# Turning attention probabilities by DMA transposes instead of TensorE, from the third pair on, in a decoder layer on one core

## What is computed

```
q, k, v = x @ wq + bq, x @ wk + bk, x @ wv + bv        # 16 heads of 16
scores  = softmax(q k^T / 4)                            # per batch row and head, 128 x 128
x = layernorm(x + (scores v) @ wo.T + bo)
x = layernorm(x + recurrence(x, ctx, w, u))             # a scan over the 128 tokens
G, I = top_k(softmax(x @ Wg.T)), K = 128 = all tokens   # 8 experts, so every token goes to every expert
x = layernorm(x + sum_e G_e * (gelu(x @ W1_e + b1_e) @ W2_e + b2_e))    # hidden width 1024
```

## Time and profile before

| | |
|---|---|
| median of 3 runs | 942.04 us (941.66 to 944.41) |
| the profiled execution's own time | 944.04 us |
| its span in the profile | 942.3 us |
| PE busy, and its share | 892.0 us, 95% |
| DVE, ACT busy | 599.3 us (64%), 579.7 us (62%) |
| mean granted clock of TensorE | 0.974 |
| DMA engines | 172.43 MB, mean 183 GB/s |

### The profile page before, as it was taken

One profiled execution on the slowest core, in us unless ns is written; L12 is line 12 of the kernel. 1 busy time (PEld: TensorE's weight loads), 2 busy tenths in 40 slices (PEclk: granted clock), 3 DMA queues, 4 the chain that ended last, 5 costly groups with the idle time before them and its releaser, 6 DMA issues.

```text
span 942.3 us, 17858 instructions
## 1 busy us (share of the span) xinstructions
PE 892.0 (95%) x6672; PEld 815.4 (87%) x6672; DVE 599.3 (64%) x1246; ACT 579.7 (62%) x991; POOL 79.2 (8%) x116
## 2 busy tenths in 40 slices
PE   4759888999999999999999999999999999999997
PEld 3659888889988988989998989889998999899997
DVE  5888879777656574665676564656756564433574
ACT  4438875786655666665566666655666665444684
POOL 2330012000110010200120001200110000000000
PEclk8669989999999999999999999999999999999999
DMA  7617999967755554555645454554545455555340
GB/s 226 211 48 247 363 349 314 316 211 247 234 179 151 172 163 144 165 169 156 187 127 177 159 183 153 151 175 156 173 131 184 148 173 167 191 192 164 114 137 12
DMA packets 144693, 172.43 MB, mean 183 GB/s; under 512 B 11208, under 2 KB 110816, under 8 KB 144608
## 3 DMA queue, kind: packets, MB, share of 16 engines
q1 hardware_dynamic: 144608, 171.29, 56.6%
HBM read 135.60 MB, written 35.65 MB: 182 GB/s over the span
## 4 chain that ended last, share of the span: by engine, by line
PE 85%; DVE 8%; ACT 4%; issue 1%; DMA 0%; POOL 0%; SPq 0%; POOLq 0%; ACTq 0%; DVEq 0%
PE down_ps L736 13%; PE down_ps L737 12%; PE down_ps L738 12%; PE up_ps L511 12%; PE up_ps L513 12%; PE up_ps L512 12%; PE bank L564 2%; PE bank L511 2%; PE bank L513 1%; PE bank L512 1%; PE bank L550 1%; PE bank L533 1%; DVE w_lo L893 1%; ACT h_all L836 1%; PE bank L582 1%
## 5 line engine op out<-in xcount | busy, mean ns | idle before, releaser
L836 ACT ACTIVATE h_all<-up_ps,b_all 128x512 f32<-128x512 f32 (+1 forms) x296 | 183.3, 635 | 256.7 <-PE up_ps L513 255.2
L893 DVE TENSOR_TENSOR h_lo<-h_all,h_hi 128x512 fp32r<-128x512 f32 x256 | 177.5, 693 | 221.3 <-ACT h_hi L827 220.8
L736 PE MATMUL down_ps<-w_hi,h_hi 128*128 128x256 f32 x1024 | 295.3, 288 | 2.9 <-DVE acc L1074 2.9
L737 PE MATMUL down_ps<-w_lo,h_hi 128*128 128x256 f32 x1024 | 289.9, 283 | 0.0
L738 PE MATMUL down_ps<-w_hi,h_lo 128*128 128x256 f32 x1024 | 289.6, 283 | 0.0
L511 PE MATMUL up_ps<-x2t_hi,w_hi 128*128 128x512 f32 (+1 forms) x592 | 222.5, 376 | 1.6 <-DVE x2t_lo L893 0.9
L513 PE MATMUL up_ps<-x2t_hi,w_lo 128*128 128x512 f32 (+1 forms) x592 | 217.1, 367 | 0.0
L512 PE MATMUL up_ps<-x2t_lo,w_hi 128*128 128x512 f32 (+1 forms) x592 | 216.3, 365 | 0.0
L736 PEld LDWEIGHTS down_ps<-w_hi,h_hi 128*128 128x128 f32 x1024 | 195.3, 191 | 11.6 <-issue 2.0
L737 PEld LDWEIGHTS down_ps<-w_lo,h_hi 128*128 128x128 f32 x1024 | 196.0, 191 | 6.8
L738 PEld LDWEIGHTS down_ps<-w_hi,h_lo 128*128 128x128 f32 x1024 | 195.8, 191 | 0.0
(11 more groups left out here) (193 smaller groups left out, 997.7 us busy)
## 6 DMA issues: line engine op xcount, KB each, us to landing
w_hi<-w_parts SPq DMA_DIRECT2D x200, 256.0 KB, 3.0
w_lo<-w_parts SPq DMA_DIRECT2D x200, 256.0 KB, 3.3
w_raw<-in_w_dram SPq DMA_DIRECT2D x96, 256.0 KB, 4.0
w_parts<-w_hi SPq DMA_DIRECT2D x64, 256.0 KB, 3.9
w_parts<-w_lo SPq DMA_DIRECT2D x64, 256.0 KB, 4.3
x_in<-in_x_dram SPq DMA_DIRECT2D x8, 256.0 KB, 3.8
ctx_sb<-in_ctx_dram SPq DMA_DIRECT2D x8, 256.0 KB, 3.9
out_dram<-acc SPq DMA_DIRECT2D x8, 256.0 KB, 2.5
```

The costliest lines, as they stand in the source:

```text
L736: nc.tensor.matmul(ps, hi, w2h[:, c, :], start=c == 0 and j == 0, stop=False, skip_group_check=True)
L737: nc.tensor.matmul(ps, hi, w2l[:, c, :], start=False, stop=False, skip_group_check=True)
L836: a = nc.scalar.activation(h_all[:, unit % HALL, k * wide:(k + 1) * wide], up_ps[unit % 2][:, k * wide:(k + 1) * wide], ACT.Gelu_apprx_tan ...
L893: return nc.vector.tensor_tensor(dst, src, hi.bitcast(F32), ALU.subtract)
```

## The change

For pairs 2 to 7 (the third on), the step T no longer runs on PE. ACT copies all eight blocks of a unit from `probs` to `p_hi` in half precision, with queries still on partitions; DVE takes the rest into `p_lo`; and SP issues two DMA transposes of 128 by 1024 half-precision elements, `pt_hi<-p_hi` and `pt_lo<-p_lo`. There is one `p_hi` and one `p_lo`, so ACT's copy of a unit waits until both transposes of the unit before have landed (`pt_loaded`). PE's value product waits for `pt_loaded`. The value product of the first unit also waits for all of the pair's shifts (`shifted`), and the scores of units 2 and 3 wait no more for `att` of the first two. The sums computed are the same. The table of steps is rewritten for these pairs:

```diff
@@ -178,6 +178,8 @@
         probs = sb("probs", [P, 2, 2, HQ, S])
         pt_hi = sb("pt_hi", [P, 2, 2, HQ, S], F16)
         pt_lo = sb("pt_lo", [P, 2, 2, HQ, S], F16)
+        p_hi = sb("p_hi", [P, 2, HQ, S], F16)
+        p_lo = sb("p_lo", [P, 2, HQ, S], F16)
...
@@ -370,6 +375,14 @@
         def second(p):
             return p == 1
 
+        def by_dma(p):
+
+            return p >= 2
+
+        def turns(p):
+
+            return UNITS * (p - 2)
+
...
+
+            def turn_probs(p, u):
+
+                if u >= 2:
+                    sp.wait_ge(pv_ps, QUADS * p + 2 * (u - 1))
+                sp.wait_ge(p_hi_ready, turns(p) + u + 1)
+                sp.dma_start_transpose(pt_hi[:, u % 2].rearrange("p i h t -> p (i h) t"),
+                                       p_hi[:].rearrange("p i h t -> p (i h t)")).then_inc(pt_loaded, 16)
+                sp.wait_ge(p_lo_ready, turns(p) + u + 1)
+                sp.dma_start_transpose(pt_lo[:, u % 2].rearrange("p i h t -> p (i h) t"),
+                                       p_lo[:].rearrange("p i h t -> p (i h t)")).then_inc(pt_loaded, 16)
...
             for n in range(VISITS):
                 for k in range(len(ITEMS[n])):
+                    for p, s in steps(FIRST_ITEM[n] + k):
+                        if s in TURN and by_dma(p):
+                            turn_probs(p, TURN.index(s))
...
+                if u == 2 and second(p):
+                    pe.wait_ge(att_ready, UNITS * p + 2)
+                if u == 2 and by_dma(p):
+                    pe.wait_ge(shifted, QUADS * p + 4)
                 if u == 2 and not first(p):
-                    pe.wait_ge(att_ready, UNITS * p + 2)
                     if second(p - 1):
...
+                if by_dma(p):
+                    if u == 0:
+                        pe.wait_ge(shifted, QUADS * (p + 1))
+                    if u >= 2:
+                        pe.wait_ge(att_ready, UNITS * p + (u - 1))
+                    pe.wait_ge(pt_loaded, 32 * (turns(p) + u + 1))
                 for i in range(2):
-                    pe.wait_ge(pt_ready, QUADS * p + (2 * u + i + 1))
+                    if not by_dma(p):
+                        pe.wait_ge(pt_ready, QUADS * p + (2 * u + i + 1))
...
-                    if s == TURN[u]:
+                    if s == TURN[u] and not by_dma(p):
                         turn_probs(p, u)
                     if s == VALUES[u]:
...
                 if part == 4:
+                    if second(b):
+                        pe.wait_ge(shifted, QUADS * (b + 1) + 4)
...
-                    if s == TURN[u]:
+                    if s == TURN[u] and by_dma(p):
+                        for i in range(2):
+                            act.wait_ge(probs_ready, QUADS * p + (2 * u + i + 1))
+                        if turns(p) + u > 0:
+                            act.wait_ge(pt_loaded, 32 * (turns(p) + u))
+                        nc.scalar.activation(p_hi[:], probs[:, u % 2], ACT.Copy).then_inc(p_hi_ready, 1)
+                    if s == TURN[u] and not by_dma(p):
...
-                            if u >= 2:
+                            if u >= 2 and not by_dma(p):
                                 dve.wait_ge(pt_ps, QUADS * p + (g - 3))
+                            if u >= 2 and by_dma(p):
+                                dve.wait_ge(p_lo_ready, turns(p) + u - 1)
...
-                    if s == TURN[u]:
+                    if s == TURN[u] and by_dma(p):
+                        dve.wait_ge(p_hi_ready, turns(p) + u + 1)
+                        nc.vector.tensor_tensor(p_lo[:], probs[:, u % 2], p_hi[:], ALU.subtract).then_inc(p_lo_ready, 1)
+                    if s == TURN[u] and not by_dma(p):
...
 JOIN = (0, 5, 9, 13, 17, 21, 25, 29)
 STEADY = {X: -66, X_LOW: -65, X_BIAS: -65, QK: -63, K_COPY: -63, Q_COPY: -63, K_LOW: -62, DIAG_0: -62, Q_LOW: -61, V: -60,
-          V_ADD: -59, V_SPLIT: -58, S_0: -57, M_0: -57, S_1: -57, M_1: -57, DIAG_1: -53, E_0: -52, E_1: -52, T_0: -49, T_1: -48, W_0: -45, W_1: -43,
-          S_2: -41, M_2: -41, S_3: -41, M_3: -41, E_2: -36, E_3: -36, T_2: -33, T_3: -32, W_2: -29, W_3: -27,
+          V_ADD: -59, V_SPLIT: -58, S_0: -57, M_0: -57, S_1: -57, M_1: -57, DIAG_1: -53, E_0: -52, E_1: -52, T_0: -51, T_1: -46,
+          S_2: -45, M_2: -45, S_3: -45, M_3: -45, E_2: -40, E_3: -40, W_0: -40, T_2: -39, W_1: -37, T_3: -34, W_2: -32, W_3: -28,
...
-     R_LOGITS: 35, R_MAX: 36, R_GATE: 41, R_GATE_T: 50, R_BIAS: 51},
-     S_0: 37, M_0: 37, S_1: 37, M_1: 37, DIAG_1: 40, E_0: 41, E_1: 41, T_0: 44, T_1: 45, W_0: 48, W_1: 49, S_2: 53, M_2: 53, S_3: 53, M_3: 53, E_2: 57, E_3: 57,
-     T_2: 60, T_3: 61, W_2: 64, W_3: 65, ATT: 68, CTX: 69, WO: 71, NORM1: 73, Y1: 76, XEXP: 76, REC_0: 76, REC_1: 77, REC_2: 79,
+     S_0: 37, M_0: 37, S_1: 37, M_1: 37, DIAG_1: 40, E_0: 41, E_1: 41, T_0: 42, T_1: 46, S_2: 48, M_2: 48, S_3: 48, M_3: 48, W_0: 52, E_2: 53, E_3: 53, T_2: 54, W_1: 53,
+     T_3: 59, W_2: 60, W_3: 64, ATT: 68, CTX: 69, WO: 71, NORM1: 73, Y1: 76, XEXP: 76, REC_0: 76, REC_1: 77, REC_2: 79,
```

More of the change, by code:

```diff
@@ L302, in decoder_layer @@
         pt_ready = sem("pt_ready")
+        p_hi_ready = sem("p_hi_ready")
+        p_lo_ready = sem("p_lo_ready")
+        pt_loaded = sem("pt_loaded")
         pv_ps = sem("pv_ps")
@@ L1252 @@
      WO: 22, NORM1: 24, Y1: 26, XEXP: 26, REC_0: 26, REC_1: 27, REC_2: 28, REC_3: 28, BACK: 31, NORM2: 31, R_TURN: 33,
-     R_LOGITS: 35, R_MAX: 36, R_GATE: 41, R_GATE_T: 50, R_BIAS: 51},
+     R_LOGITS: 35, R_MAX: 36, R_GATE: 41, R_GATE_T: 45, R_BIAS: 46},
     {X: 26, X_LOW: 27, X_BIAS: 27, QK: 29, K_COPY: 29, Q_COPY: 29, K_LOW: 30, DIAG_0: 32, Q_LOW: 32, V: 32, V_ADD: 34, V_SPLIT: 35,
-     S_0: 37, M_0: 37, S_1: 37, M_1: 37, DIAG_1: 40, E_0: 41, E_1: 41, T_0: 44, T_1: 45, W_0: 48, W_1: 49, S_2: 53, M_2: 53, S_3: 53, M_3: 53, E_2: 57, E_3: 57,
-     T_2: 60, T_3: 61, W_2: 64, W_3: 65, ATT: 68, CTX: 69, WO: 71, NORM1: 73, Y1: 76, XEXP: 76, REC_0: 76, REC_1: 77, REC_2: 79,
+     S_0: 37, M_0: 37, S_1: 37, M_1: 37, DIAG_1: 40, E_0: 41, E_1: 41, T_0: 42, T_1: 46, S_2: 48, M_2: 48, S_3: 48, M_3: 48, W_0: 52, E_2: 53, E_3: 53, T_2: 54, W_1: 53,
+     T_3: 59, W_2: 60, W_3: 64, ATT: 68, CTX: 69, WO: 71, NORM1: 73, Y1: 76, XEXP: 76, REC_0: 76, REC_1: 77, REC_2: 79,
      REC_3: 80, BACK: 84, NORM2: 85, R_TURN: 87, R_LOGITS: 89, R_MAX: 90, R_GATE: 91, R_GATE_T: 95, R_BIAS: 97}]
```

## The result

The changed kernel takes **949.18 us** (median of 20 runs, 943.65 to 954.86); the kernel before, on the same chips, 942.65 (20 runs, 941.66 to 946.11). The ratio is 1.0069 (95% interval 1.0053 to 1.0084): slower by 0.7%. The forecast was 947, its range 930 to 964. The executions also spread 11 us where those of before spread 4.5. The profiled one took 947.15 us (span 945.4), 3.1 more than that of before. One execution of run 6's kernel was slow (2939.40 us) and is left out there.

A forecast was written before the change was run, and what follows sets the result against it. PE's list of matmuls bounds the kernel, every wait at full price. -20.9 + 4.2 + 12.5 + 4.5 + 5.1 = +5.4 us gives 949.4 on the profiled execution, 947.4 on the median; forecast 947 us, range 930 to 964.

The forecast's parts named there:

- What goes: PE's list: each of six pairs loses four transpose groups of 0.87 us, 20.9 us less in all.
- GELU late: Units 0 and 1: `p_hi` ahead of ACT's second table load makes PE wait 0.7 us a pair, 4.2 us.
- Accumulators late: First down of the new visit waits for additions behind step M: 2.5 us a pair, 12.5 us for five steady pairs.
- The lag at the start of M: DVE's late start: 1.3 us from GELU through `h_lo`, 0.4 for unit 0's transposes, 0.2 for ACT behind late GELU.
- Third pair: 2.5 us for accumulators plus 2 us at its first value product, item 52, waiting for step M and shifts: 4.5 us.
- Clock: Behind waits of 2.5 us, 3.4 us at half clock, 1.7 us each in three of six pairs: 5.1 us.
- Covered: SP's held loads, the second pair's moved routing steps and the last value product cost PE nothing: 0.
- The first: Rival, faster: DVE is in time, accumulators cost 0.6 us a pair; 931, from 925 to 939, chance 0.27.
- The second: Rival, even: waits as summed but the clock holds; 942, between 939 and 945, chance 0.22.
- The third: Rival, clearly slower: transposes land late, at 5 us or more, delaying `p_hi`, step M and additions; 957 up, chance 0.18.
- The fourth: Rival, far slower: a transpose's blocks follow one another, up to 26 us a DMA; some 1,170 at 10 us, chance 0.02.
- The fifth: Rival: the change doesn't do what it says; 192 transposes gone from PE make the 20.9 us sure, no separate chance.

The follow-up runs named there:

- run 6: Run 1 with T of units 0 and 1 of the steady pairs one item later, so that ACT converts GELU ahead of `p_hi`: 932.67 us, 0.9872.
- run 12: Run 6 with the steady pairs' last value products (W_2 at -28, W_3 at -23) and steps behind them up to two items later: 928.81 us, 0.9854.
- run 1: Changed kernel with step M of units 2 and 3 of the steady pairs back behind the additions, what follows three to four items later: 933.26 us, 0.9895.
- run 2: Kernel before, transposes on PE, steady pairs' scores and step M of units 2 and 3 at item 3, first transposes and value products earlier: 955.11 us, 1.013.
- run 3: Changed kernel with two buffers each for `p_hi` and `p_lo`, so ACT's copy waits for the transposes of two units ago: 941.11 us, 0.9983.
- Run 7: Run 6 with the third pair's units 2 and 3 later too (S and M from item 48 to 53, W_0 from 52 to 57): 933.89 us, 0.9907.
- run 4: Changed kernel with 14 matmuls on constants ahead of the first down product of the five visits where steady pairs wait for accumulators: 943.82 us, 1.0006.
- run 9: Changed kernel with T of unit 0 of the third pair at item 44 instead of 42, behind the additions: 953.62 us, 1.0101.
- run 10: Run 1 and run 9 together: step M late in the steady pairs, third pair's T of unit 0 at item 44: 939.60 us, 0.9964.
- run 8: Run 7 with two buffers each of `p_hi` and `p_lo`: 932.96 us, 0.9891.
- run 5: Run 4 with the idle matmuls also in the third pair's visit (visit 5): 945.32 us, 1.0017.

## Why the prediction was right

The forecast of 947 stands 2 us under the median. The mechanism came true in the steady pairs: what PE gains it waits away, for GELU and for additions behind step M, and the clock takes its part. That 947 also meets the profiled execution's 947.15 is luck: the sum was set on the median before, on the profiled execution it gives 949.4, and there the terms come to +2.8 us instead of +5.4. Term by term:

- **What goes, 20.9 us (3.48 a pair).** Right. Three of the four periods of run 12 have no wait and take 105.20 us; before they take 108.64. The difference is 3.44. The price had to come from the chain; busy time alone shows 9.5 us less in four periods of after, where 13.8 us of matmuls are gone, since the low clock and the starts behind waits stretch what remains.
- **GELU late, 0.7 us a pair.** Right in the five steady pairs: the wait is 0.76, and run 6 takes it away by the item that the working named, `p_hi` ahead of the second table load. By periods it costs 0.98: the two of run 1 with no other wait take 106.18 us, those of run 12 without one 105.20. In the third pair it is 0.26 and 0.50, and both stand at units 2 and 3, where the working had put nothing.
- **Accumulators late, 2.5 us a pair.** A little large. The wait is 1.85 to 2.13 us. By periods it costs 108.22 (no low clock) - 106.18 (run 1) = 2.04. Of its parts, DVE's list alone, 0.6, is 0.65 in run 2. The lag at the start of M, 1.3 + 0.4 + 0.2 = 1.9, is 1.6. The 0.4 of it for the landing of unit 0's transposes is 0.2 to 0.4 by run 3. Run 1 shows the whole term to be the order of M and the additions.
- **Third pair, 4.5 us.** Near in sum, wrong in mechanism, and this is the step that failed. With GELU it was to pay 5.2; its period is 112.85 against 112.25 us, so with 3.44 gone it pays 4.0. I had charged it to step M and the value product at item 52. Run 7 moved both and the wait stayed at 3.48 us. What grew that wait is `p_lo` of unit 0, waiting for `p_hi`, ahead of the additions at item 43 (1.40 us), and a group of transposes that had stood ahead of a wait (0.87). The moved step M even took away a wait of 1.31 us at 196 us. Two things were missed. The list of waits in the earlier trace rows begins at 170 us and so leaves out the kernel before's own wait of 1.22 us at 168 us; with it in view, one of the four groups counted as gain in this pair was none. And my eyes were on the step with the largest cost, not on which new instruction stands ahead of `add_expert`.
- **Clock, 5.1 us: three pairs of six, 1.7 each.** Right in kind. Three steady pairs of five show it; a period with it takes 109.64 against 108.22 us, 1.4 each, 4.3 in all. Run 4 shows it apart from the waits. How many there are changes from one execution to the next. Only one of the twenty has a trace, with a mean granted clock of 0.968, but the clocks of all are on record: 0.967 to 0.969 in the three fastest (943.65 to 946.27 us), 0.963 in the middle, 0.960 in six that took 949.82 to 954.86. One stretch of 3.4 us at half clock is 0.0018 of the span, so the middle execution had, by that estimate, two or three more of them than the profiled one. The three of the trace are thus on the low side, and with it the term.
- **Covered: SP, loads, last value product.** Right for the changed kernel: PE waits for no weights, and for a landing only in the third pair, 0.3 us at 205 us and 1.0 us at 184 us (`issue` in the list, but the transpose lands as the wait ends). It was nearer to its edge than I wrote: in runs 1 and 6 the last value product stands five items behind its transpose instead of six, and value products wait 2.5 and 4.6 us.

With these the sum is -20.6 + 4.9 + 10.2 + 4.3 + 4.0 = +2.8 us, where the two profiled executions differ by 3.1.

**The rivals.** The first (DVE in time, 931) needed waits under 1.2 us; they are 1.9. But its time is about that of run 1, where M was put back. The second, 942 with the clock held, is in effect run 3, at 941.11. The third needed a landing of 5 us. It is 3.7 us in the middle, for 128 by 1024 elements of half precision, beside 3.3 and 3.6 us for the loads of 256 KB in the same trace; without the third pair, from 250 to 900 us, it is 3.3 and 3.4 beside 3.2 and 3.5. That agrees with the sentence of the Trainium skill, Advanced Engine Details and Errata, X-Bar Transpose (TRN2), that these are as fast as regular DMAs. The fourth needed the blocks to follow one another, up to 26 us for a DMA; eight blocks landed in 3.7 us, 0.46 each, so it is out. The Trainium skill, VectorE: DVE Perf Modes, The three transpose paths, has 1309 ns for one block, of which the prediction made an estimate of 10.5 us for eight; the measurement decides against that. The fifth is out: 192 matmuls are gone.

## What to carry to other kernels

When work leaves the engine that bounds the kernel, the gain exists only once the engines that took it over are in time at the next hand-over: look at what now stands ahead of the step that releases the bounding engine (here `add_expert`), instruction by instruction, and move it behind. One table row of items was worth 15.9 us here, and removing the last waits 4.5 more, out of a gain of 21. Before moving a step away from one wait, see which transfer it issues and what is in the queue at its new place: run 6 gave back most or all of what it removed, run 9 more than that. An instruction that is taken from ahead of a wait is no gain: begin the list of waits before the first place that the change touches. A wait of two microseconds on TensorE can cost 1.4 us more in clock, so such waits are the first to shorten.

## What the runs showed of the hardware

- **The clock beside waits near 2 us is not the same every time.** In the changed kernel waits of 1.92, 1.85 and 1.97 us were followed by 3.4 us at half clock, waits of 1.92 and 2.13 us were not. In run 9 three of 1.90 us and one of 3.76 were, one of 1.86 was not. Five waits of 1.68 to 1.70 us in run 3 were not. Waits of 2.57 us (run 6), 2.74 us (run 10) and 2.31 us (run 8) were; 1.84 in run 8, 1.86 in run 4 and 2.65 in runs 7 and 8 were not. One wait of 2.03 to 2.08 us, near 152 us, stands in all fourteen traces, and the clock fell within 2 us of its end in three (runs 5, 6 and 12). The third pair's 3.48 us stands in eight, and the clock fell behind it or in it in seven, all but the changed kernel's. I can't say from these traces what else decides.
- **70 idle matmuls made the kernel 5.4 us faster**, by the periods of run 4 through the clock alone.
- **A DMA transpose holds SP** for 1.25 to 1.35 us, against 0.4 to 0.6 for a plain one, and the second of two for up to 4.6 us when loads have just been issued; loads behind it start that much later. Its landing grows from 3.1 to 7.4 us then. In none of these kernels did PE wait for a late load behind 160 us, so the cost stays with the transposes' own readers.
